# A graph layer in four stages: eight more chunks kept between two stages, and some of the one-hots made by GpSimd

## The reference, cut to what matters

```python
total_edge = jnp.concatenate([node_feats[src], node_feats[dst], edge_feats], axis=-1)
nbr_filter = jax.nn.sigmoid(_bn(total_edge @ W1.T + b1, g1, bt1))
nbr_core = jax.nn.softplus(_bn(nbr_filter, g2, bt2))
h = nbr_filter * nbr_core
agg = jax.ops.segment_sum(h, dst, num_segments=N_NODES)
new_node = _bn(agg, g3, bt3)
return node_feats + new_node
```

## Time and profile before

| | us |
|---|---|
| median of 3 runs | 2491.14 (2486.88 to 2492.76) |
| the profiled execution | 2487.57 |
| its span, first to last instruction | 2485.8 |
| busy in the span: PE, DVE, ACT, POOL | 911.4, 1059.4, 566.3, 1745.6 |
| stage 2, from its first instruction to that of stage 3 | 1971.0 to 2100.0 |
| stage 3, to VectorE's last addition | 2100.0 to 2422.5 |

### The profile page before, as it was taken

How to read it: one execution, slowest core, us unless ns; L and a number is a source line. 1 busy time by engine, 2 the same in 40 slices (tenths; PEclk the granted TensorE clock), 3 DMA queues, 4 the chain that set the end, 5 groups by cost and what they waited for, 6 DMA issues and landing times. The chain is left out here.

```text
span 2485.8 us, 21685 instructions
## 1 busy us (share of the span) xinstructions
PE 911.4 (37%) x5728; PEld 455.0 (18%) x5728; DVE 1059.4 (43%) x1761; ACT 566.3 (23%) x536; POOL 1745.6 (70%) x1678
## 2 busy tenths in 40 slices
PE   4433233222232223222323233222232200878877
PEld 3110010000010011000100010000010000766663
DVE  4423223322233223322223223322233498999985
ACT  1100000000000000000000000000000397899965
POOL 7777777777777777777777777777777411966654
PEclk8655555555555555555555555555555555999998
DMA  9754555555555555555545555777655496888732
GB/s 268 191 122 122 132 123 122 128 131 125 124 122 123 130 125 122 129 128 128 123 121 129 124 124 122 186 202 211 164 121 129 151 377 226 296 277 279 252 93 104
DMA packets 244302, 398.19 MB, mean 160 GB/s; under 512 B 66783, under 2 KB 132125, under 8 KB 231665
## 3 DMA queue, kind: packets, MB, share of 16 engines
q1 hardware_dynamic: 138345, 284.20, 38.9%
q0 software_dynamic: 50048, 51.30, 11.5%
q10 hardware_dynamic: 55819, 61.63, 8.3%
HBM read 295.52 MB, written 101.46 MB: 160 GB/s over the span
## 5 line engine op out<-in xcount | busy, mean ns | idle before, releaser
L394 POOL DMA_INDIRECT rows<-p_table,idx x1500 | 1415.5, 944 | 457.1 <-issue 447.1
L488 PE MATMUL xg_ps<-ident,rows 128*128 128x128 f32 x564 | 156.2, 432 | 1052.5 <-DMA rows<-p_table,idx 1052.5
L546 ACT ACTIVATE z_sb<-z_ps 128x512 f32<-128x512 f32 x196 | 116.9, 596 | 1777.6 <-PE z_ps L441 1755.4
L711 DVE TENSOR_TENSOR z_sb<-z_sb,xg_ps 128x512 f32<-128x512 f32 x144 | 99.0, 688 | 760.0 <-PE xg_ps L488 760.0
L441 PE MATMUL z_ps<-into_z,with_w 128*64 128x512 f32 (+1 forms) x784 | 380.7, 1071 | 22.8 <-DMA into_z<-e_main 22.8
L488 PEld LDWEIGHTS xg_ps<-ident,rows 128*128 128x128 f32 x564 | 100.2, 215 | 1288.6 <-DMA rows<-p_table,idx 1288.6
L968 POOL TENSOR_TENSOR h_buf<-h_buf,s_all 128x1536 f32<-128x1536 f32 x66 | 223.4, 3425 | 84.6 <-ACT h_buf L940 84.6
L680 DVE TENSOR_TENSOR into_z<-d_in,node_ps 84x1024 f32<-84x1024 f32 x196 | 235.2, 1200 | 27.9 <-DMA d_in<-dst_f 27.6
L606 DVE COPY idx<-src_idx 128x16 int32 (+1 forms) x93 | 20.5, 221 | 513.1 <-PE q_ps L488 261.2
L979 PE MATMUL sum_ps<-near,h_rows 128*64 128x84 f32 x3128 | 154.4, 242 | 56.3 <-DVE agg L1031 49.7
L713 DVE BATCH_NORM_STATS2 stats<-z_sb 128x512 f32 (+1 forms) x196 | 135.6, 692 | 29.3 <-DVEq L708 2.1
(11 more groups left out here) (148 smaller groups left out, 754.2 us busy)
## 6 DMA issues: line engine op xcount, KB each, us to landing
s_all<-edge_mem SPq DMA_DIRECT2D x110, 768.0 KB, 6.7
d_in<-dst_f SPq DMA_DIRECT2D x97, 672.0 KB
edge_mem<-z_sb ACTq DMA_DIRECT2D x97, 512.0 KB, 4.7
into_z<-e_main SPq DMA_DIRECT2D x98, 336.0 KB
near<-near_mem SPq DMA_DIRECT2D x65, 504.0 KB, 4.2
near_mem<-near_one SPq DMA_DIRECT2D x97, 336.0 KB, 4.4
rows<-p_table,idx POOLq DMA_INDIRECT x1500
agg<-edge_mem SPq DMA_DIRECT2D x8, 768.0 KB
```

What stands on the lines that cost most here:

```text
L394: gp.indirect_dma_start(out=to[0:size.tile, t, h, :], out_offset=None, in_=table, in_offset=bass.IndirectOffsetOnAxis(ap=which, axis=0)).t ...
L488: mm = pe.transpose(xg_ps[s][:, t * size.tile:(t + 1) * size.tile], edges(t), eye)
L546: act.activation(z_sb[s][:, 0:size.half], z_ps[s % 2][:, 0:size.half], ACT.Copy).then_inc(e_copied, 1)
```

## The change

In stage 2, eight more chunks (`MORE`, numbers 20 to 27) get memory of their own, `more`, in the room that stage 3 uses for its buffers. SP loads them as four pairs at the start of the stage; ScalarE gates them and VectorE counts them after the eight early ones; SP writes the gates back behind all loads, in four transfers of 1536 KB, and waits for them. Stage 1 fetches chunks 28 to 39 into the slots instead of 20 to 31. `KEPT` becomes 28, so stage 3 has its batches of gates at 28, 34, ... 64.

In stage 3, GpSimd makes the one-hots of the last two chunks before each batch (26 and 27, 32 and 33, ... 62 and 63: 14 chunks), each as twelve comparisons of 128 x 84 with one scalar per partition, in the step in which ScalarE begins the batch, after its product of that step. VectorE leaves these out. TensorE waits on a counter for each of the two makers. GpSimd's usual path is written out in full, and the loops of the others begin one turn later (36 steps written out).

```diff
-    for t in range(2 * slots):
+    for t in range(3 * slots):
         step(t, t % slots, t // slots)
-    with eng.Fori(2, turns) as i:
+    with eng.Fori(3, turns) as i:
...
-        EARLY = 8
+        EARLY, MORE = 8, 8
...
-                    c = C_SLOTS + n
+                    c = C_SLOTS + n + (MORE if n >= EARLY else 0)
...
+            more_pair = [sb(f"more{n}", [P, 2 * CHUNK, HALF]) for n in range(MORE // 2)]
+            more = [more_pair[n // 2][:, n % 2 * CHUNK:(n % 2 + 1) * CHUNK] for n in range(MORE)]
...
-            MAIN_CHUNKS = CHUNKS - S - EARLY
+            MAIN_CHUNKS = CHUNKS - S - FIRST
...
+                for n in range(MORE // 2):
+                    sp.dma_start(more_pair[n][:], chunk_pair(n)).then_inc(more_loaded[n], 16)
                 for n in range(EARLY):
                     sp.wait_ge(gated, n + 1)
                     sp.dma_start(chunk_of(S + n), early[n]).then_inc(s_kept, 16)
                 in_order(sp, load)
                 sp.dma_start(s_buf_r[:], edge_mem_r).then_inc(r_loaded, 16)
+                for n in range(MORE // 2):
+                    sp.wait_ge(gated, EARLY + 2 * n + 2)
+                    sp.dma_start(chunk_pair(n), more_pair[n][:]).then_inc(more_kept, 16)
                 sp.wait_ge(s_kept, 16 * EARLY)
+                sp.wait_ge(more_kept, 16 * (MORE // 2))
...
+                for n in range(MORE):
+                    if n % 2 == 0:
+                        act.wait_ge(more_loaded[n // 2], 16)
+                    act.activation(more[n], more[n], ACT.Sigmoid, scale=bn1[:, 0:1], bias=bn1[:, 1:2]).then_inc(gated, 1)
...
+                for n in range(MORE):
+                    v.wait_ge(gated, EARLY + n + 1)
+                    for k in range(CHUNK):
+                        ins = v.bn_stats(stats[:, (S + EARLY + n) * CHUNK + k, :], more[n][:, k, :])
+                    ins.then_inc(s_counted, 1)
...
-            H, BATCH, KEPT = 6, 6, C_SLOTS + EARLY
+            H, BATCH, KEPT = 6, 6, C_SLOTS + EARLY + MORE
...
+            AHEAD = (BATCH + KEPT - 2) % BATCH, (BATCH + KEPT - 1) % BATCH
+
+            def by_pool(m):
+
+                return m.slot % BATCH in AHEAD and (not isinstance(m.c, int) or m.c >= KEPT - 2)
...
+                    if (m := back(0)) and m.slot % BATCH == KEPT % BATCH and not ready(m) and not general:
+                        for k in (2, 1):
+                            m = back(k)
+                            gp.wait_ge(summed, (m.c - 1) * CHUNK)
+                            places = rel[:, m.c * CHUNK:(m.c + 1) * CHUNK, TILES:]
+                            for j in range(CHUNK * TILES):
+                                g, t = j // TILES, j % TILES
+                                hots = gp.tensor_scalar(near_by_half[m.slot % 2][:, g, 1, t], iota_row[:], places[:, g, t:t + 1], None, ALU.is_equal)
+                            hots.then_inc(near_by_pool, 1)
...
+                with gp.If(rare < 1):
+                    for t in range(CHUNKS + 2):
+                        step(lambda k: Item(t - k, (t - k) % S, (t - k) // S) if 0 <= t - k <= CHUNKS else None, False)
...
-                            pe.wait_ge(near_ready, m.c + 1)
+                            if by_pool(m):
+                                pe.wait_ge(near_by_pool, by_pool_till(m) + 1)
+                            else:
+                                pe.wait_ge(near_ready, by_vector_till(m) + 1)
...
-                        if m := hots:
+                        if (m := hots) and not by_pool(m):
```

More of the change, by code:

```diff
@@ L758, in build @@
             s_buf_r = sb("s_buf_r", [P, T_HALF])
-            S = C_SLOTS
+            more_pair = [sb(f"more{n}", [P, 2 * CHUNK, HALF]) for n in range(MORE // 2)]
+            more = [more_pair[n // 2][:, n % 2 * CHUNK:(n % 2 + 1) * CHUNK] for n in range(MORE)]
+            more_loaded = [sem(f"more_loaded{n}") for n in range(MORE // 2)]
+            more_kept = sem("more_kept")
+            S, FIRST = C_SLOTS, EARLY + MORE
             stats = sb("stats2", [P, GROUPS + 1, 6])
@@ L768, in build @@
             ones_set, high_steps, high_set, highs = (sem(n) for n in ("ones_set", "high_steps", "high_set", "highs"))
-            MAIN_CHUNKS = CHUNKS - S - EARLY
+            MAIN_CHUNKS = CHUNKS - S - FIRST
             def in_order(eng, body):
-                rounds(eng, MAIN_CHUNKS, S, lambda n, s, turn: body(n, n + S + EARLY, s, turn))
+                rounds(eng, MAIN_CHUNKS, S, lambda n, s, turn: body(n, n + S + FIRST, s, turn))
                 for c in range(S):
@@ L791, in load, with chunk_pair @@
                         return
-                    after(sp, s_counted, EARLY + last_in_slot(n, c) + 1)
+                    after(sp, s_counted, FIRST + last_in_slot(n, c) + 1)
                     sp.dma_start(s_in[s], chunk_of(c)).then_inc(z_loaded[s], 16)
+                def chunk_pair(n):
+                    return edge_mem[(S + EARLY + 2 * n) * CHUNK:(S + EARLY + 2 * n + 2) * CHUNK].rearrange("k p w -> p k w")
+                for n in range(MORE // 2):
+                    sp.dma_start(more_pair[n][:], chunk_pair(n)).then_inc(more_loaded[n], 16)
                 for n in range(EARLY):
@@ L829, in _ @@
                     ins.then_inc(s_counted, 1)
+                for n in range(MORE):
[3 more added lines that the diff above has]
+                    ins.then_inc(s_counted, 1)
                 def count(n, c, s, turn):
-                    v.wait_ge(gated, EARLY + n + 1)
+                    v.wait_ge(gated, FIRST + n + 1)
                     for k in range(CHUNK):
@@ L903, in ready, with by_pool_till, by_vector_till @@
                 return isinstance(m.c, int) and m.c < KEPT
+            near_by_pool = sem("near_by_pool")
+            AHEAD = (BATCH + KEPT - 2) % BATCH, (BATCH + KEPT - 1) % BATCH
+            def by_pool(m):
+                return m.slot % BATCH in AHEAD and (not isinstance(m.c, int) or m.c >= KEPT - 2)
+            PER_TURN = 2 * S // BATCH
+            SKIPPED = sum(c % BATCH in AHEAD for c in range(KEPT - 2))
+            def by_pool_till(m):
+                if isinstance(m.c, int):
+                    return sum(c % BATCH in AHEAD for c in range(max(m.c, KEPT - 2)))
+                return m.turn * PER_TURN + sum(c % BATCH in AHEAD for c in range(m.slot))
+            def by_vector_till(m):
+                if isinstance(m.c, int):
+                    return m.c - by_pool_till(m) + SKIPPED
+                return m.turn * (S - PER_TURN) + m.slot - sum(c % BATCH in AHEAD for c in range(m.slot)) + SKIPPED
             blk = stage.enter_context(nc.Block())
@@ L963, in _ @@
                 gp.iota(win_start[:], [[WIN, WINDOWS]], base=0, channel_multiplier=0, allow_small_or_imprecise_dtypes=True).then_inc(cleared, 1)
+                gp.sem_inc(near_by_pool, SKIPPED)
                 def step(back, general):
@@ L968, in step @@
                         gp.tensor_tensor(m.cols(h_buf[m.slot % H]), m.cols(h_buf[m.slot % H]), m.cols(s_in[m.slot]), ALU.mult).then_inc(h_ready, 1)
-                by_path(gp, 1, step)
+                    if (m := back(0)) and m.slot % BATCH == KEPT % BATCH and not ready(m) and not general:
[7 more added lines that the diff above has]
+                            hots.then_inc(near_by_pool, 1)
+                rare = gp.value_load(flag3[:], min_val=0, max_val=1)
+                with gp.If(rare < 1):
+                    for t in range(CHUNKS + 2):
+                        step(lambda k: Item(t - k, (t - k) % S, (t - k) // S) if 0 <= t - k <= CHUNKS else None, False)
+                with gp.Else():
+                    pipeline(gp, S, 1, lambda back: step(back, True))
+                gp.nop()
             @blk.tensor
```

## The result

| | before | after |
|---|---|---|
| median of 6 runs each, us | 2490.74 (2486.88 to 2493.43) | 2531.52 (2530.10 to 2535.68) |
| ratio, 95% interval | | 1.0162 (1.0151 to 1.0173) |
| profiled execution, its span, us | 2487.57, 2485.8 | 2530.68, 2528.5 |
| second stage, us | 128.98 | 139.45 |
| third stage, to VectorE's last addition, us | 322.48 | 350.91 |

The change makes the kernel 40.8 us slower. The forecast was 2488.0 us, with a range up to 2503; it was wrong, and so was the sign. Second stage: +10.5 us. Third stage: +28.4 us. The 1.9 us that are left of the medians' difference lie in the first stage and behind the third.

What follows compares the result with a forecast made beforehand. VectorE and DMA were taken to bound stage two closely, VectorE then ScalarE stage three. Terms of -3.6 (third stage), 0 to the stores and 0.5 held back gave -3 us from median 2491.14: 2488.0 us, range 2483 to 2503.

Steps and rivals of the forecast that it cites:

- Loads and stores of the second stage: Second stage: added stores of 6.29 MB just hidden behind VectorE's statistics and coefficients; 0 us, bounds 0 and +3.
- Loads are 37 + 8 instead of 45: Second stage: step counting 37 slot loads plus 8 kept-chunk loads in place of 45, VectorE's statistics staying without a hole.
- A hole at 2100: End of the second stage: listed as a sign that the forecast is wrong.
- waits of VectorE in the second stage: Second stage: listed as a sign that the forecast is wrong; VectorE was expected unchanged there.
- Eight more ready chunks: Third stage: ScalarE loses 15.8 us of work; first gates move to 2209.5 us, seven batches follow at 30.66 us each.
- The price of a comparison: Third stage, GpSimd: one 128x84 one-hot operation costs 0.25 us, 3.0 us a chunk; two-input price 0.36 us.
- The loop: Third stage: one-hots, product and sums take 28.3 us a batch, below ScalarE's 30.66; lateness gone by chunk 58.
- The forecast's own sum: Third stage, per batch: 12 x 0.25 one-hots, 3.4 product, 1.3 to first copy, four steps, 0.9: 28.3 us.
- the rival of a dear one-hot: Third stage: loop 24 x price + 21.6 us; +7 us at 0.36, +22 us (2513) at 0.45; 28 in 100.
- the threshold of 0.27 us: Third stage: GpSimd one-hot price above which the lateness of the products is no longer worked off.
- TensorE's clock: Third stage: after waits TensorE runs partly at 1.2 instead of 2.4 GHz, coming each time with waits in every batch.
- the step of 6.5 us: Third stage: first, slowed VectorE step of each batch, including TensorE's lower clock; 4.7 us if the clock stays at 2.4 GHz.

Runs made afterwards that it cites:

- e6: After, with the last twelve reloads in the order slots come free and all one-hots by VectorE: 2797.14 us against before's 2800.53, ratio 0.9987.
- e3: After, with only the last twelve reloads reordered to start at the slot that comes free first: 2831.14 us against before's 2800.53, ratio 1.0104.
- e14: The kernel of e6 run again on a chip with the usual first stage: 2485.72 us against before's 2487.98, ratio 0.9990.
- e1: After, with the eight more kept chunks but all one-hots by VectorE, reload order as in the change: 2807.97 us against before's 2800.53, ratio 1.0029.
- e9: After, with reloads reordered and each chunk's twelve GpSimd comparisons replaced by one 128x1008 subtraction (wrong results): 2799.65 us against before's 2807.38, third stage 318.38.
- e11: After, with reloads reordered and one 128x1008 comparison with a constant per chunk on GpSimd (wrong results): 2483.92 us against before's 2488.86, one run.
- e10: After, with reloads reordered and GpSimd's twelve comparisons made against a constant (wrong results): 2819.84 us against before's 2807.38, one run; third stage 334.36.
- e12: After, with reloads reordered and GpSimd's one-hots made by a wide subtraction, then a wide comparison with 0: 2502.80 us against before's 2488.86, ratio 1.0057.

## Why the prediction was wrong

**Loads and stores of the second stage.** I counted loads, stores and bytes, and took 0 with bounds of 0 and +3. The failed step is "Loads are 37 + 8 instead of 45", which took their order as unchanged in effect, without a reason. Not the bytes but 37 mod 12 decided, and I never worked out which count each reload waits for. It cost 9.2 us (VectorE's aggregation starts 127.03 us after the stage's start, 117.79 before; 2101.44 and 2088.79 in the next rows).

```profile
2101.44 5.46 DVE L1365 BATCH_NORM_AGGREGATE tmp<-stats 128x2 f32<-128x1176 f32 x1
```

```profile
2088.79 5.46 DVE L1302 BATCH_NORM_AGGREGATE tmp<-stats 128x2 f32<-128x1176 f32 x1
```

The first is of after, the second of before. Another 1.2 us lie behind it: the stores went out late, and the third stage begins 12.42 us after the aggregation instead of 11.19. What I had said of the stores themselves was right: in e6 and e3, without the hole, they cost 0.2 and 0.0 us, and in e14, e6's kernel again, nothing. "A hole at 2100" and "waits of VectorE in the second stage" stood among the signs of a wrong forecast; the place was 2063 to 2075.

**Eight more ready chunks.** Right. In after the first batch's table load is 109.7 us behind the third stage's start (2223.55 and 2113.86), as forecast (2209.5 - 2100.0). Alone, with seven batches of 30.66 us, the chunks give 2.4 to 2.9 us (e1, e6), close to my -3.6 for both parts together. That VectorE is rid of 14 one-hots adds at most 1.4 us to it: e9 and e11 end at 318.4 and 318.2 us, e6 at 319.6. So with a cheap operation in the same place both parts together give 4.1 and 4.3 us.

**The price of a comparison.** This is the larger miss. The term was 0.25 us, from the one-input affine select of 128x128 (0.292 us), with 0.36 as the upper end. Measured: 0.471 us from one to the next, and 0.500 of busy time, which is what the rows behind 0.25 and 0.36 give. The 0.36 was no bare scaling by columns: 0.455 us at 128 columns less 44 x 2.14 ns holds a fixed part of 0.18 us. So a missing fixed part is not the reason. By busy time the comparison with a constant takes 0.422 us at 84 columns and 2.729 at 1008, that is 2.50 ns a column and 0.21 us fixed. Of the 0.14 us above my upper end, 0.06 is this, an operation dearer than the two-input product in both parts, and 0.08 is the scalar per partition (0.422 to 0.500; 0.086 from one to the next). For the scalar I had no row and put nothing on top of the upper end. VectorE's work beside it is not what makes it dear: all 168 comparisons take 482 to 517 ns.

**The loop.** Its form was right and its result missed through the price. 24 x 0.471 + 21.6 = 32.9 us a batch, and 32.9 is what six batches took. The first comparison began 128.7 us after the stage's start, forecast 128.4. The forecast's own sum, 12 x price + 25.3, is the longer one for cheap operations, and holds there: 27.2 us at e9's 0.156 and 28.0 at e11's 0.227, where the first three batches take 26.7 to 27.0 and 28.2 to 28.6. By 28 in 100 I gave the rival of a dear one-hot, +22 us at 0.45; it happened, at 0.471, with +28.4. Its two points, +7 at 0.36 and +22 at 0.45, lie on a line that gives +11 at 0.385, where e10 shows 334.4 - 322.5 = +12, and +25.5 at 0.471; the last 2.9 us are in no term. I gave no working for the threshold of 0.27 us, and the runs only enclose it: hidden at 0.16 and 0.23 (e9 and e11, a twelfth of their chunk), not at 0.385.

**Sum.** +10.5 and +28.4 are 38.9 of the 40.8 us. The range could not hold it, since its upper end cut the dear rival at 0.38 us and no case had the hole.

**TensorE's clock.** The stretch of the third stage shows a mean of 0.90 against 0.97, as TensorE waits 59.3 us for products. I had forecast this for waits in every batch, in the step of 6.5 us. No run has it apart, so what it costs stays open.

## What to carry to other kernels

When the number of turns of a ring of slots changes, work out for each load in an in-order queue which count it waits for, and let the epilogue go on at the slot that is next in turn. Before handing work to an engine that looks idle, find the wait that must stand ahead of it and what is queued behind that wait: here the same twelve operations cost 25 us in one place and nothing one step earlier. A price taken from another operation by its columns is no upper bound, even with its fixed part, and each operand of another kind wants a price of its own; where the whole result turns on it, keep the range open to twice as much.

## What the runs showed of the hardware

A one-input comparison on GpSimd is dearer than a two-input subtraction of the same 128x1008 tile: 2.73 us in e11 and e12 alike (2.50 ns a column and a fixed part) against 1.88 us in e9 (at most 1.86 ns a column). I had taken one input to be the cheaper kind. The Trainium skill, "GPSIMD Engine Reference", Engine selection, has one-input work roughly at line rate and two-input work about twice as slow as on VectorE; for the comparison the trace does not agree, as VectorE makes one-hots of that size, from two inputs, in 1.21 us, and the measurement decides. The prediction's estimate of 0.2 to 0.3 us from that page's cycles does not hold either, against 0.385 and 0.471. The same page's section Performance pitfalls gives about 102 cycles for a read command that does not overlap, an estimate of 0.085 us at its clock of 1.2 GHz; the 0.086 us that the scalar per partition adds is of that size, though no run here shows that this is its cause.
